# A sandwich block on one core: the last layer norm's mean folded into the down weights, and a token's two expert rows added by an accumulating transfer

## The chip, the core and the metric

One Trainium2 chip, one of its cores. The metric is the device time of one launch in microseconds (us). TensorE multiplies, VectorE, ScalarE and GpSimd work element by element, SyncE only issues transfers; each of them runs its own list of instructions in order and waits on semaphores for the others. GpSimd can issue transfers too, on a queue of its own.

## The reference

The input is x of 8 batches of 256 rows of 256 channels: 2048 tokens, which the kernel holds as 16 tiles of 128 tokens.

```python
x = x + layernorm(attention(layernorm(x)))       # 16 heads, 4 kv heads, D 128, rope, causal
x = x + layernorm(ffn(layernorm(x)))

# ffn, for each token
probs = softmax(xf @ gate_w.T);  w, idx = top_k(probs, 2);  w = w / w.sum()
h = silu(xf @ w_gate[e]) * (xf @ w_up[e])        # 8 experts, 176 wide
out = sum over the two chosen e of w_e * (h_e @ w_down[e])
out += sigmoid(xf @ shgate_w) * (silu(xf @ shw_gate) * (xf @ shw_up) @ shw_down)   # shared, 352 wide

layernorm(y) = (y - mean(y)) / sqrt(var(y) + 1e-5)
```

Everything is float32. The last step of the output is thus a layer norm over the 256 channels of the sum of three rows (two experts' and the shared one), added to x.

## The kernel before

Matmuls run in float32 replaced by three products of high and low parts (`mm3`, L468 to L472). The work has four stages.

1. Attention, up to about 480 us. A loop over steps s = 0 to 128 (`WOVEN`) writes each engine's order out; a step holds one head of one batch, and even and odd steps alternate between a light and a heavy part of the projection and rope. 16 steps are a batch. GpSimd applies rope (L1982, L1985, L1992), VectorE the other element-wise work. SyncE fills the table `xs` with zeros meanwhile, loads the shared weights `sw` and, as their places come free, the experts' weights `ew` (`load_ew`, L425), gate, up and down of an expert in one transfer; the down part of the shared weights is the third part of `sw` (L423).
2. Shared expert for tiles 0 to 10 ("U" items), and the scatter of every token's row to the two lists of its experts.
3. Routed experts: 39 tiles ("R" items) of 128 listed rows. Each result row is multiplied by its weight (L1138) and scattered by GpSimd to `ys` (L2105), where the first and the second choice of a token lie next to each other (1 KB each).
4. The tail, from 634 us. TensorE computes the shared expert of tiles 11 to 15: `u_gate`, `u_up`, `u_T`, `u_down`. ScalarE multiplies the result by the token's gate (`u_out`, L1101). When the last rows of `ys` have landed, SyncE loads eight pairs of tiles, each with both choices (L453 to L457, 512 KB each). For pairs 0 to 4 GpSimd adds the choices (`last_ysum`, L2108) and VectorE the shared rows (`last_sum`, L1709). For pairs 5, 6 and 7 TensorE adds all three in PSUM by multiplying with the identity (`pair_results`, L766; `pair_shared`, L777). VectorE takes mean and variance (`last_stats`, L1716, then `norm_aggr`), GpSimd the reciprocal root and the negative mean times root (`last_root`, L2039), ScalarE applies both (`last_apply`, L1140; for pair 7 VectorE, L1729), VectorE adds to x (L1740, L1735), and SyncE stores (L460, L463).

The order in stages 3 and 4 comes from `ffn(q)`, one function for each engine (L782, L1147, L1743, L2113), called for item after item; `PAIR`, `PPE` and `PSUM` say at which item which pair is treated.

Of the kernel before, what the change touches and what calls it, by code (L numbers as in the profile page):

```python
# [11 lines left out]
NB = 8  # L12
# [5 lines left out]
NE = 8  # L18
# [41 lines left out]
YRING = 4  # L60


U0 = 139
# [17 lines left out]
PAIR = {U1 + 3 + p: p for p in range(NPAIR)}  # L81
SEND = U1 + 3 + NPAIR + 4

PPE = 5
PSUM = U1 + NT - UFIRST + 1
# [30 lines left out]
def program(nc, x_d, wqkv_d, wo_d, gb_d, sw_d, ew_d, cs_d, const_d, route_d, spare_d, out_d):  # L116
    with ExitStack() as ctx:
# [14 lines left out]

        def part(t, at, n):
            return t[:, at:at + n]
# [31 lines left out]
        rs = sb("rs", [128, 2, 5])  # L166
        half = sb("half", [128, 8])
# [36 lines left out]

        ew_raw = [part(ropes, z * EH, EH) for z in range(3)]
# [8 lines left out]
        for c, (a, b) in enumerate(CHUNKS):  # L214
# [62 lines left out]
                for (a, b), p in zip(CHUNKS, (pQ[:, 768:1024], pS[1], pS[1]))]  # L277
# [9 lines left out]
        pSum = [pS[1], pA, pT]  # L287
# [8 lines left out]
        s_dsw, s_droute, s_zeroed = sem("s_dsw"), sem("s_droute"), sem("s_zeroed")  # L296
        s_dew = [sem(f"s_dew{z}") for z in range(2)]
# [3 lines left out]
        s_dyl = [sem(f"s_dyl{p}") for p in range(NPAIR)]  # L301
        s_out = sem("s_out")
# [17 lines left out]
        s_shared, s_y, s_fapp = (sem(n) for n in ("s_shared", "s_y", "s_fapp"))  # L320
# [24 lines left out]
        s_add, s_mul, s_rope, s_swlo, s_shalf, s_zrow, s_weq, s_wsel, s_ysum = (  # L345
            sem(n) for n in ("s_add", "s_mul", "s_rope", "s_swlo", "s_shalf", "s_zrow", "s_weq",
                             "s_wsel", "s_ysum"))
# [20 lines left out]
        def root_of(p):  # L368

            return p // 2 if p < 6 else p - 3  # L370
# [18 lines left out]
        block = ctx.enter_context(nc.Block())  # L389

        @block.sync
        def _(e):
# [18 lines left out]
            e.dma_start(rc, route_d).then_inc(s_droute, 16)  # L411
            e.wait_ge(s_zrow, 1)
# [8 lines left out]
            e.dma_start(part(stage, UB, 2 * SHUP), sw_d[:, 0:2 * SHUP]).then_inc(s_dsw, 16)  # L421
            e.wait_ge(s_swlo, 2)
            e.dma_start(sw_raw[2], sw_d[:, 2 * SHUP:]).then_inc(s_dsw, 16)  # L423

            def load_ew(x):  # L425
                if x >= 2:
                    e.wait_ge(s_dew[x % 2], 16 * (x // 2))
# [39 lines left out]
        def _(e):  # L467
# [298 lines left out]
            def pair_results(p):  # L766
                e.wait_ge(s_dyl[p], 16)
                if p == PPE:
                    e.wait_ge(s_y, NRT)
                elif p == PPE + 1:  # L770
                    e.wait_ge(s_rlo, NRT)
                else:
                    e.wait_ge(s_usilu, NT)
                e.matmul(pair_row[p], ident, yl[p][:, :, 0:HID], start=True, stop=False, skip_group_check=True)
                e.matmul(pair_row[p], ident, yl[p][:, :, HID:2 * HID], start=False, stop=False, skip_group_check=True)

            def pair_shared(p):  # L777
                e.wait_ge(s_shared, 2 * p + 2)
                e.matmul(pair_row[p], ident, shpair[p].rearrange("p (t c) -> p t c", t=2), start=False, stop=True,
                         skip_group_check=True).then_inc(s_psum, 1)  # L780

            def ffn(q):  # L782
# [4 lines left out]
                if q == U1:  # L787
                    r_T(h)
                    r_down(g)
                    r_down(h)  # L790
                elif kind == "U":
                    u_gate(i)
                if q == PSUM:
                    pair_results(PPE)
                if before2 == "U" and q > U1:
                    u_down(g)
                if before == "U" and q > U1:
                    u_T(h)
                if kind == "U":
                    u_up(i)  # L800
# [8 lines left out]
                if q == U1 - 1:  # L809
                    u_gate(UFIRST)  # L810
                if q == PSUM:
                    pair_shared(PPE)
                    for p in range(PPE + 1, NPAIR):
                        pair_results(p)
                        pair_shared(p)
# [134 lines left out]
            for q in range(R0 + 1, SEND):  # L950
                ffn(q)

        @block.scalar
        def _(e):
# [85 lines left out]
            def ew_hi(x):  # L1040
                e.wait_ge(s_dew[x % 2], 16 * (x // 2 + 1))
# [59 lines left out]
            def u_out(m):  # L1101
# [4 lines left out]
                elif m == 14:  # L1106
                    e.wait_ge(s_shalf, 2)
# [32 lines left out]
            def last_apply(p):  # L1140
                e.wait_ge(s_nb2, NB + root_of(p) + 1)
# [1152 lines left out]
```

## Time and profile before

| | us |
|---|---|
| three runs | 671.63, 672.00, 673.67 |
| median | 672.0 |
| the profiled execution: its own time | 673.56 |
| the profiled execution: its span, first to last instruction | 671.8 |

| engine | busy us | share of the span |
|---|---|---|
| TensorE (PE) | 631.1 | 94% |
| ScalarE (ACT) | 551.3 | 82% |
| VectorE (DVE) | 549.9 | 82% |
| GpSimd (POOL) | 530.5 | 79% |

The profile names engines PE, PEld (TensorE's weight load), DVE, ACT, POOL and SP; SPq is SyncE's transfer queue; L12 is line 12 of the kernel. An instruction's duration overlaps with its follower's beginning, so that the step from one start to the next is shorter than the duration.

### The profile page before, as it was taken

How to read it: one execution, taken by the hardware profiler on the slowest of the kernel's cores; microseconds unless marked ns; L12 is line 12 of the kernel's file. 1: busy time of each engine (PE TensorE's matmuls, PEld its weight loads, DVE VectorE, ACT ScalarE, POOL GpSimd, SP SyncE). 2: the span in 40 equal slices, each digit the busy share in tenths (PEclk: the TensorE clock that was granted, in tenths of full speed). 3: DMA queues.
4: the chain of work that ended last, by engine and by line, in shares of the span. 5: the costliest groups of instructions: out<-in, count | busy, mean ns of one | idle time of the engine just before them, and what ended most of it. 6: DMA issues, size and time to landing. Idle time of an engine off the chain costs nothing.

```text
span 671.8 us, 15617 instructions
## 1 busy us (share of the span) xinstructions
PE 631.1 (94%) x4506; PEld 586.9 (87%) x4506; DVE 549.9 (82%) x1912; ACT 551.3 (82%) x2105; POOL 530.5 (79%) x601
## 2 busy tenths in 40 slices
PE   5879999999999999999999999999789989999993
PEld 5657899999999999999999999999678889999991
DVE  3989999898898889899898999979878755555466
ACT  3589999999999999999999999999787536666633
POOL 3698898999899899989989998999757424666664
PEclk9999999999999999999999999999899999999997
DMA  8001306997740000000000000000526033444173
GB/s 328 33 0 33 104 1 198 335 335 209 4 47 1 1 1 1 1 1 2 1 1 1 1 1 2 1 1 25 160 101 229 33 90 111 128 130 119 67 265 125
DMA packets 51122, 54.27 MB, mean 81 GB/s; under 512 B 19840, under 2 KB 42752, under 8 KB 50912
## 3 DMA queue, kind: packets, MB, share of 16 engines
q1 hardware_dynamic: 47632, 43.90, 23.6%
q0 software_dynamic: 3408, 9.38, 3.7%
q8 instruction: 39, 0.64, 0.4%
q14 instruction: 43, 0.35, 0.2%
HBM read 23.83 MB, written 29.51 MB: 79 GB/s over the span
## 4 chain that ended last, share of the span: by engine, by line
PE 75%; DVE 9%; POOL 5%; issue 4%; ACT 4%; DMA 2%; POOLq 0%; SPq 0%; ACTq 0%; DVEq 0%
PE pQ L470 8%; PE pQ L471 8%; PE pQ L472 8%; PE pPO L576 5%; PE pPO L470 5%; PE pPO L472 5%; PE pPO L471 5%; PE pT L548 4%; PE pSS L470 3%; PE pA L470 3%; PE pA L471 3%; PE pA L472 3%; PE pSS L471 2%; PE pSS L472 2%; POOL xs L2076 2%
## 5 line engine op out<-in xcount | busy, mean ns | idle before, releaser
L1002 ACT ACTIVATE P<-P,nmx 128x128 f32<-128x128 f32 (+1 forms) x256 | 118.8, 491 | 1.0 <-DVE nmx L1445 1.0
L470 PE MATMUL pQ<-W 128*128 128x512 f32 (+2 forms) x334 | 116.1, 347 | 2.4 <-DVE W L1359 1.2
L471 PE MATMUL pQ<-W 128*128 128x512 f32 (+2 forms) x334 | 111.6, 334 | 0.0
L472 PE MATMUL pQ<-W 128*128 128x512 f32 (+2 forms) x334 | 111.3, 333 | 0.0
L1982 POOL TENSOR_TENSOR ropes<-ropes 128x640 f32<-128x640 f32 x63 | 99.3, 1576 | 13.7 <-DVE ropes L1422 13.4
L1010 ACT ACTIVATE P<-P,rinv 128x128 f32<-128x128 f32 (+1 forms) x256 | 105.8, 481 | 2.1 <-DVE rinv L1451 2.1
L1992 POOL TENSOR_TENSOR ropes<-ropes 128x640 f32<-128x640 f32 x63 | 99.6, 1580 | 4.9
L470 PE MATMUL pPO<-W 128*128 128x256 f32 (+1 forms) x323 | 95.3, 295 | 5.6 <-DVE W L1460 3.9
L987 ACT ACTIVATE ropes<-pQ 128x128 f32<-128x128 f32 x320 | 88.4, 303 | 9.7 <-PE pQ L472 9.7
L471 PE MATMUL pPO<-W 128*128 128x256 f32 (+1 forms) x323 | 92.0, 285 | 0.0
L472 PE MATMUL pPO<-W 128*128 128x256 f32 (+1 forms) x323 | 91.8, 284 | 0.0
L1455 DVE TENSOR_TENSOR W<-pPO,W 128x384 fp32r<-128x384 f32 x128 | 70.2, 548 | 23.5 <-ACT W L1015 23.4
L1985 POOL TENSOR_TENSOR ropes<-ropes,rs 128x640 f32<-128x640 f32 x63 | 80.3, 1274 | 4.9
L1968 POOL TENSOR_TENSOR rs<-rs,half 128x5 f32<-128x5 f32 x64 | 76.0, 1187 | 5.3
L987 ACT ACTIVATION_READ_ACCUMULATOR ropes<-pQ 128x1 f32 x320 | 74.8, 237 | 0.0
L470 PEld LDWEIGHTS pPO<-W 128*128 128x128 f32 x323 | 62.0, 192 | 12.0 <-DVE W L1460 6.1
L470 PEld LDWEIGHTS pQ<-W 128*128 128x128 f32 x334 | 63.4, 190 | 6.6 <-DVE W L1359 1.6
L1015 ACT ACTIVATE W<-pPO 128x384 fp32r<-128x384 f32 x128 | 65.9, 515 | 2.9 <-PE pPO L576 2.9
L472 PEld LDWEIGHTS pQ<-W 128*128 128x128 f32 x334 | 63.2, 189 | 5.6
L1432 DVE TENSOR_TENSOR W<-pT,W 128x384 fp32r<-128x384 f32 (+1 forms) x128 | 61.6, 481 | 5.6 <-ACT W L995 5.5
L2105 POOL DMA_INDIRECT ys<-ropes x39 | 38.8, 995 | 34.2 <-ACT ropes L1138 28.7
L471 PEld LDWEIGHTS pQ<-W 128*128 128x128 f32 x334 | 63.4, 190 | 2.6
(272 smaller groups left out, 2170.5 us busy)
## 6 DMA issues: line engine op xcount, KB each, us to landing
xs<-stage SPq DMA_DIRECT2D x1, 17550.0 KB, 58.4
stage<-xs SPq DMA_DIRECT2D x39, 130.0 KB
ropes<-in_ew SPq DMA_DIRECT2D x8, 608.0 KB
stage<-in_wqkv SPq DMA_DIRECT2D x3, 768.0 KB, 9.0
stage<-ys SPq DMA_DIRECT2D x4, 512.0 KB, 7.3
ropes<-ys SPq DMA_DIRECT2D x4, 512.0 KB, 6.8
out<-X SPq DMA_DIRECT2D x7, 256.0 KB, 2.0
X<-in_wo SPq DMA_DIRECT2D x1, 1536.0 KB, 12.7
```

The costliest lines, as they stand in the source:

```text
L470: e.matmul(out, lh, rh, start=start, stop=False, skip_group_check=True)
L471: e.matmul(out, lh, rl, start=False, stop=False, skip_group_check=True)
L472: return e.matmul(out, ll, rh, start=False, stop=stop, skip_group_check=True)
L987: a = e.activation(t2[:, z, h * D:h * D + D], pQ[:, h * D:h * D + D], ACT.Square, accum_out=ss[:, z, h:h + 1])
L1002: a = e.activation(P[:, z, span(t)], P[:, z, span(t)], ACT.Exp, bias=nmx[:, z, t:t + 1], scale=-1.0, accum_out=sums[:, z, t:t + 1])
L1010: a = e.activation(P[:, z, span(t)], P[:, z, span(t)], ACT.Copy, scale=rinv[:, z, t:t + 1])
L1015: e.activation(PT[:, 0, n % 2, :], pP[:, 0:384], ACT.Copy).then_inc(s_PThi, 1)
L1455: e.tensor_tensor(PT[:, 1, n % 2, :], pP[:, 0:384], f(PT[:, 0, n % 2, :]), ALU.subtract).then_inc(s_PT, 1)
L1968: e.tensor_tensor(dst, dst, half[:, 0:n], ALU.pow).then_inc(s_root, 1)
L1982: e.tensor_tensor(t1[:, z3, :], t1[:, z3, :], t2[:, z, :], ALU.add).then_inc(s_add, 1)
L1985: e.tensor_tensor(v3, v3, rs[:, z, :].unsqueeze(2).to_broadcast([128, 5, D]), ALU.mult).then_inc(s_mul, 1)
L1992: e.tensor_tensor(v3, v3, TB[:, t, :, :], ALU.add).then_inc(s_rope, 1)
```

## The change

1. Down weights without a mean. SyncE loads the down weights of the shared expert (parts of 512 and 256 columns) and of the eight experts (512 columns) one part at a time into a free piece of `ropes`; VectorE takes the sum of each row of 256 (`down_mean`, steps 48, 56, ..., 120) and subtracts sum/256 (`down_centre`, steps 50, 58, ..., 122); SyncE writes the part to a new table `downs` in device memory. `load_ew` is now two transfers for each expert, gate and up from the input, down from `downs`, and the third part of `sw` comes from `downs` as well. Each row of the sum of the three results then has the mean zero, and the last layer norm needs only the mean of squares.
2. The choices. SyncE loads the first choices of a pair (256 rows of 1 KB), and GpSimd issues a transfer which adds the second choices to them (`second_choice`, `accum_op=ALU.add`), in the order 0, 1, 2, 3, 6, 4, 7, 5. The transfer o waits for the transfer o-2 to land. GpSimd's sums (`last_ysum`) are gone.
3. Pairs 6 and 7 on TensorE. The token's gate is multiplied in by VectorE before the down product (`u_act`), `u_down` of tiles 12 to 15 writes straight into the pair's PSUM bank, and one identity product adds the choices. Pairs 0 to 5 take the shared rows by VectorE.
4. The norm. ScalarE squares the pair's rows with an accumulated sum (`last_square`), GpSimd takes the root in four groups (pairs 0-1, 2-3, 4-6, 7), VectorE does x + row * root in one instruction for each tile (`last_add`). `last_stats`, `last_apply` and `last_scale` are gone.
5. The tail's order is written out as a list for every engine, from item `U1`.

```diff
+CHOICE = (0, 1, 2, 3, 6, 4, 7, 5)
+
+
+DOWN = [(NE, 0, 2 * HID), (NE, 2 * HID, NKT * HID)] + [(x, EA, EH) for x in range(NE)]
+DOWN_SUM = {48 + 8 * c: c for c in range(len(DOWN))}
+DOWN_SUB = {50 + 8 * c: c for c in range(len(DOWN))}
...
-PAIR = {U1 + 3 + p: p for p in range(NPAIR)}
-SEND = U1 + 3 + NPAIR + 4
-
-PPE = 5
-PSUM = U1 + NT - UFIRST + 1
+PPE = 6
+NSUM = 2 * PPE
...
-        pSum = [pS[1], pA, pT]
+        pSum = [pS[1], pA]
...
-            return p // 2 if p < 6 else p - 3
+            return min(p // 2, 2) if p < NPAIR - 1 else 3
...
+        def choice_rows(p, k):
+            return ys_d[4 * 128 * p:4 * 128 * (p + 1), :].rearrange("(t p k) c -> p t k c", t=2, k=2)[:, :, k, :]
+
+        def wait_choices(e, p):
+            o = CHOICE.index(p)
+            e.wait_ge(s_dyl2[o % 2], 16 * (o // 2 + 1))
...
+            def load_down(c):
+                x, a, b = DOWN[c]
+                src = ew_d[:, x * EH + a:x * EH + b] if x < NE else sw_d[:, 2 * SHUP + a:2 * SHUP + b]
+                e.dma_start(down_raw[c % 2][:, 0:b - a], src).then_inc(s_ddown, 16)
+
+            load_down(0)
...
+            for c in range(len(DOWN)):
+                x, a, b = DOWN[c]
+                at = 2 * x * HID + (a if x == NE else 0)
+                e.wait_ge(s_down, 2 * c + 1)
+                if c > 0:
+                    e.wait_ge(s_sdown, 16 * c)
+                if c + 1 < len(DOWN):
+                    load_down(c + 1)
+                e.wait_ge(s_down, 2 * c + 2)
+                e.dma_start(downs_d[:, at:at + b - a], down_raw[c % 2][:, 0:b - a]).then_inc(s_sdown, 16)
             e.wait_ge(s_swlo, 2)
-            e.dma_start(sw_raw[2], sw_d[:, 2 * SHUP:]).then_inc(s_dsw, 16)
+            e.wait_ge(s_sdown, 16 * len(DOWN))
+            e.dma_start(sw_raw[2], downs_d[:, NE * 2 * HID:]).then_inc(s_dsw, 16)
...
-                e.dma_start(ew_raw[x % 3], ew_d[:, x * EH:(x + 1) * EH]).then_inc(s_dew[x % 2], 16)
+                e.dma_start(ew_raw[x % 3][:, 0:EA], ew_d[:, x * EH:x * EH + EA]).then_inc(s_dew[x % 2], 16)
+                e.dma_start(ew_raw[x % 3][:, EA:EH], downs_d[:, x * 512:x * 512 + 512]).then_inc(s_dew[x % 2], 16)
...
-            for p in range(NPAIR):
-                if p == 6:
-                    e.wait_ge(s_hU, NOWN)
-                e.dma_start(yl[p], ys_d[4 * 128 * p:4 * 128 * (p + 1), :].rearrange(
-                    "(t p k) c -> p t (k c)", t=2, k=2)).then_inc(s_dyl[p], 16)
+            e.wait_ge(s_hU, NOWN)
+            for p in CHOICE:
+                e.dma_start(yl[p][:, :, 0:HID], choice_rows(p, 0)).then_inc(s_dyl[p], 16)
...
-                else:
+                elif m < NSUM:
                     e.wait_ge(s_shared, m)
                 if m == UFIRST:
                     e.wait_ge(s_y, NRT)
+                elif m == NSUM + 2:
+                    e.wait_ge(s_rlo, NRT)
+                out = pair_row[m // 2][:, m % 2, :] if m >= NSUM else pD
                 for k in range(NKT):
-                    p = mm3(pD, [aTs[m % 2][:, i, k * 128:k * 128 + 128] for i in range(2)],
-                            [shdown_w(i, k) for i in range(2)], k == 0, k == NKT - 1)
+                    p = mm3(out, [aTs[m % 2][:, i, k * 128:k * 128 + 128] for i in range(2)],
+                            [shdown_w(i, k) for i in range(2)], k == 0 and (m < NSUM or m % 2 == 0), k == NKT - 1 and m < NSUM)
...
             def pair_results(p):
+                wait_choices(e, p)
+                e.matmul(pair_row[p], ident, yl[p][:, :, 0:HID], start=False, stop=True,
                          skip_group_check=True).then_inc(s_psum, 1)
 
...
+            u_gate(15)
+            u_down(13)
+            u_T(14)
+            u_up(15)
+            u_T(15)
+            u_down(14)
+            pair_results(6)
+            u_down(15)
+            pair_results(7)
...
-            def last_apply(p):
-                e.wait_ge(s_nb2, NB + root_of(p) + 1)
+            def last_square(p):
+                if p < PPE:
+                    e.wait_ge(s_fsum, p + 1)
+                else:
+                    e.wait_ge(s_psum, p - PPE + 1)
+                if p < 4:
+                    e.wait_ge(s_nb2, NB)
+                else:
+                    e.wait_ge(s_lr2, NB + root_of(p - 4) + 1)
                 for t in range(2):
-                    a = e.activation(yl[p][:, t, 0:HID], pair_row[p][:, t, :], ACT.Identity, bias=nb2[:, p % 4, t:t + 1],
-                                     scale=lr2[:, p % 4, t:t + 1])
-                a.then_inc(s_fapp, 1)
-
-            def ffn(q):
+                    a = e.activation(yl[p][:, t, HID:2 * HID], pair_row[p][:, t, :], ACT.Square,
+                                     accum_out=mv2[:, p % 4, t, 1:2])
+                a.then_inc(s_ssq, 1)
...
+            u_silu(14)
+            u_hi(13)
+            last_square(0)
+            u_silu(15)
+            u_hi(14)
+            last_square(1)
+            u_hi(15)
+            last_square(2)
+            last_square(3)
+            last_square(4)
+            last_square(5)
+            last_square(6)
+            last_square(7)
...
+            def down_rows(c):
+                x, a, b = DOWN[c]
+                return down_raw[c % 2][:, 0:b - a].rearrange("p (k d) -> p k d", d=HID), (b - a) // HID
+
+            def down_mean(c):
+                rows_c, n = down_rows(c)
+                e.wait_ge(s_ddown, 16 * (c + 1))
+                e.tensor_reduce(down_sum[:, c, 0:n], rows_c, AXX, ALU.add).then_inc(s_down, 1)
+
+            def down_centre(c):
+                rows_c, n = down_rows(c)
+                e.wait_ge(s_down, 2 * c + 1)
+                e.scalar_tensor_tensor(rows_c, down_sum[:, c, 0:n].unsqueeze(2).to_broadcast([128, n, HID]), -1.0 / HID,
+                                       rows_c, ALU.mult, ALU.add).then_inc(s_down, 1)
...
-                e.tensor_tensor(actb[m % 2][:, 0:NSH], sgb[m % 2], pU, ALU.mult).then_inc(s_uact, 1)
+                if m < NSUM:
+                    e.tensor_tensor(actb[m % 2][:, 0:NSH], sgb[m % 2], pU, ALU.mult).then_inc(s_uact, 1)
+                else:
+                    e.wait_ge(s_shalf, 1 if m < 14 else 2)
+                    e.scalar_tensor_tensor(actb[m % 2][:, 0:NSH], sgb[m % 2], sgate[:, m:m + 1], pU, ALU.mult,
+                                           ALU.mult).then_inc(s_uact, 1)
...
             def last_sum(p):
-                e.wait_ge(s_ysum, p + 1)
+                wait_choices(e, p)
                 e.wait_ge(s_shared, 2 * p + 2)
                 e.tensor_tensor(yl[p][:, :, 0:HID], yl[p][:, :, 0:HID], shpair[p].rearrange("p (t c) -> p t c", t=2),
                                 ALU.add).then_inc(s_fsum, 1)
-                e.wait_ge(s_fsum, p + 1)
-
...
+            def last_add(p):
...
+                    x = X[:, 2 * p + t, :]
+                    a = e.scalar_tensor_tensor(x, pair_row[p][:, t, :], lr2[:, p % 4, t:t + 1], x, ALU.mult, ALU.add)
+                    if t == 1 or p == NPAIR - 1:
+                        a.then_inc(s_fres, 1)
...
+            u_lo(13)
+            last_sum(0)
+            u_act(14)
+            last_sum(1)
+            u_lo(14)
+            u_act(15)
+            last_sum(2)
+            u_lo(15)
+            last_sum(3)
+            last_add(0)
+            last_add(1)
+            last_sum(4)
+            last_sum(5)
+            last_add(2)
+            last_add(3)
+            last_add(4)
+            last_add(5)
+            last_add(6)
+            last_add(7)
...
             def last_root(p, n):
                 k = NB + root_of(p)
                 if p >= 4:
-                    e.wait_ge(s_fapp, p + n - 4)
+                    e.wait_ge(s_fres, p + n - 4)
                 else:
                     e.wait_ge(s_h2row, NT)
                 z = slice(p % 4, p % 4 + n)
-                e.wait_ge(s_aggr2, NB + p + n)
-                e.tensor_scalar(lr2[:, z, :], mv2[:, z, :, 1], 1.0, EPS, ALU.mult, ALU.add).then_inc(s_var2, 1)
-                if p < NPAIR - 1:
-                    e.tensor_scalar(nb2[:, z, :], mv2[:, z, :, 0], -1.0, None, ALU.mult)
+                e.wait_ge(s_ssq, p + n)
+                e.tensor_scalar(lr2[:, z, :], mv2[:, z, :, 1], 1.0 / HID, EPS, ALU.mult, ALU.add).then_inc(s_var2, 1)
                 e.wait_ge(s_var2, k + 1)
                 e.tensor_tensor(lr2[:, z, :], lr2[:, z, :], half[:, 0:2 * n].rearrange("p (a b) -> p a b", a=n),
                                 ALU.pow).then_inc(s_lr2, 1)
-                if p < NPAIR - 1:
...
-            def last_ysum(p):
+            def second_choice(p):
+                o = CHOICE.index(p)
                 e.wait_ge(s_dyl[p], 16)
-                e.tensor_tensor(yl[p][:, :, 0:HID], yl[p][:, :, 0:HID], yl[p][:, :, HID:2 * HID],
-                                ALU.add).then_inc(s_ysum, 1)
-
-            def ffn(q):
+                if o >= 2:
+                    e.wait_ge(s_dyl2[o % 2], 16 * (o // 2))
+                e.dma_start(yl[p][:, :, 0:HID], choice_rows(p, 1), accum_op=ALU.add).then_inc(s_dyl2[o % 2], 16)
+
...
+            for p in CHOICE:
+                second_choice(p)
+            last_root(0, 2)
+            last_root(2, 2)
+            last_root(4, 3)
+            last_root(7, 1)
...
```

## Rows read from the trace of the kernel before

**Rows 1.** Windows of the span: length, then busy us per engine, clock, DMA share, GB/s.

```profile
core 0: us, PE busy (x) PEld busy (x) DVE busy (x) ACT busy (x) POOL busy (x), PEclk, DMA share, GB/s
...
140.00:420.00 280.00, 280.00 (x2072) 265.09 (x2071) 251.52 (x941) 268.47 (x1124) 257.42 (x271) 1.00 0.17 30
...
660.00:672.00 12.00, 1.06 (x3) 0.19 (x1) 6.64 (x17) 3.16 (x7) 5.06 (x10) 0.63 0.36 131
```

**Rows 2.** Timeline of VectorE in the attention stage: start us, us, what, idle before.

```profile
117.78 0.75 DVE L1470 BATCH_NORM_STATS2 st<-osb 128x6 f32<-128x256 f32 x2
...
202.94 0.75 DVE L1335 BATCH_NORM_STATS2 st<-X 128x6 f32<-128x256 f32 x2
203.72 0.25 DVE L1339 BATCH_NORM_AGGREGATE mv<-st 128x2 f32<-128x6 f32 x2
...
207.63 0.69 DVE L1460 TENSOR_TENSOR W<-pA,W 128x512 fp32r<-128x512 f32 x1 [0.67 <-ACT W L1021]
```

**Rows 3.** Waits within 140 to 420 us: in total us, times, longest.

```profile
POOL ropes L1982 <- DVE ropes L1422: 4.8, 5, 1.1
```

**Rows 4.** VectorE line L1464 (duration ns min/median/max), and timelines at 67 and 205 us.

```profile
L1464 DVE TENSOR_TENSOR W<-X,W x8: 680/1326/1661, 47.7 to 75.1; 128x512 fp32r<-128x512 f32 x8
...
67.48 1.33 DVE L1464 TENSOR_TENSOR W<-X,W 128x512 fp32r<-128x512 f32 x1
...
68.34 1.59 POOL L1985 TENSOR_TENSOR ropes<-ropes,rs 128x640 f32<-128x640 f32 x1
...
205.51 1.26 POOL L1985 TENSOR_TENSOR ropes<-ropes,rs 128x640 f32<-128x640 f32 x1
```

**Rows 5.** Timeline of SyncE's DMA queue: start us, us to issue, what.

```profile
182.87 4.69 SPq L421 DMA_DIRECT2D stage<-in_sw  x1
454.40 0.33 SPq L423 DMA_DIRECT2D stage<-in_sw  x1
```

**Rows 6.** The chain that ended last, its tail: start us, us, what.

```profile
637.86 2.41 DMA ys<-ropes
...
640.36 3.61 DMA stage<-ys
```

**Rows 7.** GpSimd line L2105: duration ns min/median/max, first and last start us.

```profile
L2105 POOL DMA_INDIRECT ys<-ropes x39: 954/961/1097, 560.9 to 637.9; - x39
```

**Rows 8.** Windows of the tail, columns as in Rows 1.

```profile
646.00:652.00 6.00, 5.68 (x42) 5.37 (x42) 5.83 (x16) 1.91 (x6) 5.92 (x5) 1.00 1.05 393
```

**Rows 9.** Timeline of GpSimd in the tail.

```profile
651.50 0.52 POOL L2047 TENSOR_SCALAR lr<-mv 128x4 f32<-128x4 f32 x1
...
652.30 1.04 POOL L2051 TENSOR_TENSOR lr<-lr,half 128x4 f32<-128x4 f32 x1
```

**Rows 10.** Timeline of VectorE in the tail.

```profile
647.50 0.51 DVE L1557 TENSOR_TENSOR stage<-stage,pSS 128x352 f32<-128x352 f32 x1
...
653.39 0.68 DVE L1712 TENSOR_TENSOR ropes<-ropes 128x512 f32<-128x512 f32 x1
...
666.94 0.76 DVE L1735 TENSOR_TENSOR X<-X,stage 128x256 f32<-128x256 f32 x2
```

**Rows 11.** Timeline of TensorE in the tail.

```profile
648.83 0.49 PE L687 MATMUL pPO<-const,stage 128*128 128x128 f32 x3
...
654.89 1.02 PE L779 MATMUL pSS<-P,const 128*128 128x512 f32 x2
```

**Rows 12.** Timeline of ScalarE: activations with an accumulated sum, 256 and 128 columns.

```profile
201.07 0.51 ACT L1002 ACTIVATE P<-P,nmx 128x256 f32<-128x256 f32 x1
...
201.57 0.80 ACT L1010 ACTIVATE P<-P,rinv 128x128 f32<-128x128 f32 x2
202.26 0.27 ACT L987 ACTIVATE ropes<-pQ 128x128 f32<-128x128 f32 x1
...
202.51 0.28 ACT L987 ACTIVATE ropes<-pQ 128x128 f32<-128x128 f32 x1
```

**Rows 13.** SyncE line L460, the result's seven stores of a pair: us to landing.

```profile
DMA to landing us min/median/max: 2.0/2.0/2.2
```

More of the change, by code:

```diff
@@ L202, in program @@
         rw_raw = rc[:, 215:215 + 2 * NR].rearrange("p (k r) -> p k r", k=2)
+        down_raw = [part(ropes, 2304 + 512 * z, 512) for z in range(2)]
         ew_raw = [part(ropes, z * EH, EH) for z in range(3)]
@@ L301, in program @@
         s_dyl = [sem(f"s_dyl{p}") for p in range(NPAIR)]
+        s_dyl2 = [sem(f"s_dyl2{p}") for p in range(2)]
         s_out = sem("s_out")
@@ L319, in program @@
                              "s_rhi"))
-        s_shared, s_y, s_fapp = (sem(n) for n in ("s_shared", "s_y", "s_fapp"))
+        s_shared, s_y, s_ssq = (sem(n) for n in ("s_shared", "s_y", "s_ssq"))
         s_bn, s_aggr, s_hrow, s_hT, s_wqlo, s_tab_d, s_rope_d = (
@@ L786, in ffn @@
                 after, k = item(q + 1)
[L787 to L800, printed above, removed]
                 if after == "R":
@@ L808, in ffn @@
                         r_down(g)
[L809 to L815, printed above, removed]
             centre(0)
@@ L949, in _ @@
             u_down(10)
-            for q in range(R0 + 1, SEND):
-                ffn(q)
+            for q in range(R0 + 1, U1):
+                routed(q)
+            u_gate(11)
+            r_T(NRT - 1)
+            r_down(NRT - 2)
+            r_down(NRT - 1)
+            u_up(11)
+            u_gate(12)
+            u_T(11)
+            u_up(12)
+            u_gate(13)
+            u_down(11)
+            u_T(12)
+            u_up(13)
+            u_gate(14)
+            u_down(12)
+            u_T(13)
+            u_up(14)
+            u_gate(15)
[7 more added lines that the diff above has]
+            pair_results(7)
         @block.scalar
@@ L1326, in _ @@
             u_out(10)
-            for q in range(R0 + 1, SEND):
-                ffn(q)
+            for q in range(R0 + 1, U1):
+                routed(q)
+            r_out(NRT - 3)
+            r_hi(NRT - 1)
+            u_silu(11)
+            r_out(NRT - 2)
+            r_out(NRT - 1)
+            u_silu(12)
+            u_hi(11)
+            u_silu(13)
+            u_out(11)
+            u_hi(12)
+            u_silu(14)
[11 more added lines that the diff above has]
+            last_square(7)
         @block.vector
@@ L1746, in ffn @@
                 after, k = item(q + 1)
-                if q == U1:
-                    r_lo(h)
-                if q in PAIR:
-                    if PAIR[q] < PPE:
-                        last_sum(PAIR[q])
-                    last_stats(PAIR[q])
-                if before == "U" and q > U1:
-                    u_lo(h)
-                if kind == "U":
-                    u_act(i)
                 if after == "R":
@@ L1762, in ffn @@
                     r_act(i)
-                p = PAIR.get(q - 2, 0)
-                if 0 < p < 6 and p % 2 == 1:
-                    last_add(p - 1)
-                    last_add(p)
-                elif p == 6:
-                    last_add(p)
-                elif p == 7:
-                    last_scale(p)
-                    for t in range(2):
-                        last_add_tile(p, t)
             ln1_stats(0)
@@ L1957, in _ @@
             r_act(0)
-            for q in range(R0 + 1, SEND):
-                ffn(q)
+            for q in range(R0 + 1, U1):
+                routed(q)
+            r_lo(NRT - 1)
+            u_act(11)
+            u_lo(11)
+            u_act(12)
+            u_lo(12)
+            u_act(13)
+            u_lo(13)
[17 more added lines that the diff above has]
+            last_add(7)
         @block.gpsimd
@@ L2219, in _ @@
             r_select(0)
-            for q in range(R0 + 1, SEND):
-                ffn(q)
+            for q in range(R0 + 1, U1):
+                routed(q)
+            r_out(NRT - 3)
+            r_out(NRT - 2)
+            r_out(NRT - 1)
+            for p in CHOICE:
[4 more added lines that the diff above has]
+            last_root(7, 1)
 def kernel(**inputs):
```

95 lines of the change are left out of this document (16 added, 79 removed).

## The prediction

> **What bounds the kernel now.** I read the windows of the whole span first. The reader is to see that between 140 and 420 us TensorE has no idle time (280.00 of 280) while VectorE is busy for 251.5 us of it and GpSimd for 257.4, and that after 660 us TensorE works 1.06 us of 12 [rows 1]. So the kernel is bound by TensorE nearly to the end, and then by a chain through the other engines, which the chain of waits shows: GpSimd's last scatter at 637.86 lands at 640.27, the first pair (512 KB) is issued at 640.36 and landed 3.61 us later [rows 6], and VectorE's last addition runs from 666.94 to 667.70 [rows 10]. After it come only the last stores and the end of the program. Nothing else of the change can shorten the time: it lies in the tail, and what it adds earlier must be hidden under TensorE. So I ask two things: what the added work costs before 634 us, and when VectorE's last addition would end.
>
> **Added in the attention stage.** A step lasts 3.55 us: the statistics at 117.78 belong to step 30 and those at 202.94 to step 54, so 85.16 us are 24 steps [rows 2]. The first sum (step 48) is then due at 182 us, the last centring (step 122) at 444 us. Ten row sums and ten centrings, nine of each on 512 columns. For a sum I take 0.6 us, the 0.69 of a 512-column operation of VectorE less its overlap [rows 2]. A centring reads two operands from on-chip memory; the nearest row is L1464, 512 columns with both operands there, at 0.68 to 1.66 us, median 1.33 [rows 4]. Ten times 0.6 and 1.33 are 19 us at most, against 280 less 251.5, that is 28.5 us, of idle VectorE. Is it idle in the right place? Step 54 carries statistics and aggregates of 1.0 us, and in the pair of steps behind them VectorE still waits 0.67 us for ScalarE [rows 2]: a pair has room for 1.67, and sum and centring go to different pairs. Both fit, a centring of 1.66 just so. The ends of this cost: 0 if all is hidden; if nothing of the centrings' second half could be caught up on (each 1.66 less 0.67), 10 us. I take 0.2 us, near nothing, because extras of 1.0 us leave TensorE at 280 of 280.
> GpSimd pays too. Beside the L1464 at 67.48 its multiplication at 68.34 took 1.59 us [rows 4]; the same instruction at 205.51 took 1.26 [rows 4], so a centring costs GpSimd some 0.3 us, ten of them 3 us. Over 280 us GpSimd waited for VectorE five times, 4.8 us in all [rows 3]. That cover is just enough; where it is gone, rope comes late and TensorE waits for it (a rival, below).
> The Trainium skill bears on this (page "SBUF — State Buffer", section "Who interferes with whom"): a VectorE instruction with two SBUF inputs contends with a GpSimd instruction that reads SBUF, while on trn2 a tensor_reduce never does. The row agrees for the first half (1.33 against 0.68 us); no row here shows the second. By the page the ten sums are free for GpSimd and the ten centrings aren't, which speaks against the second half of this part alone, and leaves the sum as it is.
>
> **SyncE's queue.** The first part is loaded before the zero fill. The second is issued behind the shared weights, whose issue ends at 182.87 + 4.69 = 187.6 us [rows 5], and is wanted at step 56, 210 us: hidden. Later loads and stores (256 KB; a store of that size lands in 2.0 us [rows 13]) have 28 us for each part. The last part is centred at 444 to 446 us and stored by 449; the load of the third part of the shared weights, which now waits for that store, is issued at 454.40 anyway [rows 5], because it waits for GpSimd's split. So this new wait has 5 us of slack. The split of the experts' loads adds eight issues of under 0.5 us where nobody waits for these loads. 0.
>
> **Removed from the tail.** GpSimd's five sums, seven of TensorE's nine identity products, all statistics and aggregates of VectorE, ScalarE's eight pairs of applications but for eight pairs of squares, GpSimd's negated means. What is late next is the second choices.
>
> **The chain of the accumulating transfers.** The first load is now 256 KB. The half that falls away takes 262 KB / 393 GB/s = 0.67 us at the rate of this stretch [rows 8], so it lands at 640.36 + 3.61 - 0.67 = 643.3. GpSimd then issues with g each, and a transfer lands R after its issue begins. Since transfer o waits for o-2, they go two by two in four rounds: the sixth lands at 643.3 + g + 3R, and GpSimd has issued the eighth at 643.3 + 2g + 3R. GpSimd's roots stand behind these eight issues in its list, and VectorE's last_add(0) and (1), which need the first root, stand before last_sum(4): so the whole end of the tail hangs on that moment.
> For g I take 0.96 us, as an indirect scatter of 128 rows takes [rows 7]; with 256 rows it could be double, 1.9. For R no row of before has an accumulating transfer. From below: a scatter of 128 KB lands 2.41 us after GpSimd begins it [rows 6]. From above: g and a load of 512 KB, since the transfer has to read both addends, 0.96 + 3.61 = 4.57 [rows 6, 7]. (Below nothing it can't go: it is time until data land.) I take the middle, 3.5, as neither row is nearer: the one has half the bytes, the other both addends' bytes and a neighbour in the queue. Then GpSimd is free at 643.3 + 1.9 + 10.5 = 655.7.
> From there: root of pairs 0-1, 1.5 us (651.50 to 653.34, less the 0.3 us of the negated mean) [rows 9]: 657.2. Four additions of 256 columns at 0.38 (two in 0.76) [rows 10]: 658.7. last_sum(4), 0.7 [rows 10]: 659.4. ScalarE's squares: with accumulated sum 256 columns step 0.50 us from on-chip memory (201.07 to 201.57), 128 columns from PSUM 0.25 (202.26 to 202.51) [rows 12], so I take 1.0 us for each of pairs 4 and 5 and 0.75 for pair 6: 662.2. Root of pairs 4 to 6, 1.5: 663.7. Eight additions for pairs 4 to 7, 3.0: 666.7. Six handovers of 0.05: 667.0. Pair 7's own square and root (0.75 and 1.2) run beside these additions. Before, it was 667.70: 0.7 us gained. Four pairs now store within 3 us, where each store alone takes 2.0 us [rows 13]: I add 0.2 us. Sum: -0.7 + 0.2 + 0.2 = -0.3 us on the span of 671.8.
> Does the earlier part hold? last_sum(0) stands before u_act(14) in VectorE's list and now waits for the first accumulating transfer, 643.3 + 3.5 = 646.8, done 647.5; u_act(14) began at 647.50 and TensorE came for it at 648.83 [rows 10, 11]. With R above 4.3 TensorE is held up; by then the chain above is later still, so it adds nothing. TensorE's list ends with pair_results(7), whose transfer lands at 643.3 + 4R = 657.3; before, TensorE had its last u_down done at 654.89 [rows 11] and the rest of its sums by 661. Not on the path.
>
> **In the metric.** The profiled execution took 673.56 us, its span 671.8, and the median of the three runs is 672.0; the difference of -0.3 us is laid on the median: 671.7 us. Within 0.3% (2.0 us) a measurement of this kernel can't tell a change from none; so this is a forecast of no measurable change, 0.42, with a range of its own from 670.2 to 673.2 (R from 3.0 to 4.0).
>
> **Rivals.**
> A. Short rounds, 0.30. The transfers behave like the small scatter, R = 2.4. For it: two are in flight at once, and nothing else needs the transfer engines after the loads. Against it: twice the bytes, and a read of the destination. 3 x 1.1 = 3.3 us less: 668.4 us, faster. The Trainium skill has a price here (page "DMA: Bandwidth & Descriptors", section "Anatomy of one DMA — SWDGE (gpsimd) path"): about 2.0 us plus bytes / 436e9, thus an estimate of 2.6 us for 256 KB. By that price the sum would be 669.0 us. The trace's scatter, 2.41 us with 128 KB, agrees; that page has no accumulation in this price.
> B. Long rounds, 0.20. R = 4.57, because the engines read the sum's place too or the issue of 256 rows takes 1.9 us. For it: every microsecond of R counts three times, of g twice. Against: only the upper rows have it. 3.2 us more: 674.9 us; with the long issue 676.8. It decides from R = 4.3 on (2.0 us over no change).
> C. The attention stage isn't hidden, 0.08. GpSimd's 3 us of contention fall where it had no wait (five waits for ten centrings), rope is late, TensorE waits: 674.9 us. Against: the windows show TensorE without idle time beside GpSimd at 257.4 of 280.
>
> **The numbers.** The predicted time is the likeliest case's, 671.7. Faster by over 0.3%: A and a little of the main case, 0.33. Within: 0.40, the main case with a small part of B and C less what it gives to either side. Slower: the rest of B and C, 0.27. The range, 8 in 10, reaches down to A's 668.4 less a little, and up to halfway between B's two values: 668.0 to 676.0.
>
> **What would show it.** GpSimd's eight issues two by two, the distance from the first of a round to the next is R; the first root begins at about 655.7; VectorE waits before last_add(0) and ends near 667.0. TensorE's windows from 180 to 440 us stay without idle time and its steps keep 3.55 us; the centrings show 0.7 to 1.7 us. The load of the shared down part stays at about 454 us. I am wrong if the rounds aren't two by two in effect (the loads late, the issue long), if the first root isn't what VectorE waits for, or if the routed stage begins later than before.

## The result and the profile after

| | kernel before | kernel after |
|---|---|---|
| median, us | 672.84 (4 runs, 671.63 to 677.22) | 683.84 (4 runs, 681.51 to 683.97) |
| ratio, 95% interval | | 1.0146 [1.0119, 1.0172] |
| span of the profiled execution, us | 671.8 | 682.0 |

Slower by 1.5%, above the range that was forecast. The spans differ by 10.2 us, and the tail holds nearly all of it. The first view is SyncE's timeline: the loads of the first choices begin at 641.79 us, where those of before began at 640.36 [rows 6], 1.43 us later.

```profile
641.79 0.91 SPq L489 DMA_DIRECT2D stage<-ys  x2
...
645.29 0.47 SPq L489 DMA_DIRECT2D ropes<-ys  x1
...
668.18 8.44 SPq L492 DMA_DIRECT2D out<-X  x7
```

GpSimd's timeline of the same stretch holds the eight issues of the accumulating transfers (L2152; x2 is two in one row) and behind them the roots. The brackets give the idle time before a row and what ended it.

```profile
644.64 2.58 POOL L2152 DMA_DIRECT2D stage<-ys  x2 [4.46 <-DMA stage<-ys]
652.96 1.18 POOL L2152 DMA_DIRECT2D ropes<-ys  x1 [5.74 <-DMA stage<-ys]
655.03 1.19 POOL L2152 DMA_DIRECT2D ropes<-ys  x1 [0.89 <-DMA stage<-ys]
657.95 1.18 POOL L2152 DMA_DIRECT2D stage<-ys  x1 [1.72 <-DMA ropes<-ys]
659.97 1.19 POOL L2152 DMA_DIRECT2D ropes<-ys  x1 [0.85 <-DMA ropes<-ys]
662.61 1.18 POOL L2152 DMA_DIRECT2D stage<-ys  x1 [1.45 <-DMA stage<-ys]
664.64 1.20 POOL L2152 DMA_DIRECT2D ropes<-ys  x1 [0.85 <-DMA ropes<-ys]
665.92 0.19 POOL L2091 TENSOR_SCALAR lr<-mv 128x4 f32<-128x4 f32 x1
```

The reader is to see four rounds of two. From the first round to the second it is 8.3 us, from there on 5 and 4.7; the root begins at 665.92. The chain that ended last runs through exactly these transfers (start, us, what):

```profile
641.79 2.55 DMA stage<-ys
644.34 0.30 issue
644.64 0.84 POOL stage L2152
645.47 9.05 DMA stage<-ys
...
654.56 0.47 issue
655.03 4.43 DMA ropes<-ys
...
659.50 0.47 issue
659.97 4.15 DMA ropes<-ys
...
664.64 1.19 POOL ropes L2152
```

VectorE waits 7.09 us for that root and ends at 676.18 + 0.86 = 677.04, where it ended at 667.70 before [rows 10]:

```profile
652.46 0.69 DVE L1767 TENSOR_TENSOR stage<-stage,ropes 128x512 f32<-128x512 f32 x1 [4.17 <-DMA stage<-ys]
...
667.27 1.67 DVE L1774 SCALAR_TENSOR_TENSOR X<-stage,lr,X 128x256 f32<-128x256 f32 x4 [7.09 <-POOL lr L2093]
...
676.18 0.86 DVE L1774 SCALAR_TENSOR_TENSOR X<-pA,lr,X 128x256 f32<-128x256 f32 x2
```

From SyncE's first load of the choices to VectorE's end it is 35.25 us, before 27.34. I call this the interval and use it below, since it does not depend on when the tail begins, which differs by some us from chip to chip. It repeats well: experiment 2, whose tail is the same, has 35.58 us in another batch. The 10.2 us are then 1.43 (the loads begin later), 7.91 (the interval) and 0.86 (from VectorE's end to the end of the span, 4.96 against 4.1).

### The profile page after: what moved, and what is told of

It is laid out like the page before. It is cut to its first block, busy times and chain, and to the rows that moved or that the text cites. A ratio compares the mean times of both kernels' runs of the same rounds, so it can differ in the third digit from the quotient of the medians.

```text
span 682.0 us, 15628 instructions
## 1 busy us (share of the span) xinstructions
PE 630.0 (92%) x4492; PEld 586.9 (86%) x4492; DVE 554.8 (81%) x1906; ACT 550.4 (81%) x2119; POOL 532.2 (78%) x594
## 3 DMA queue, kind: packets, MB, share of 16 engines
q1 hardware_dynamic: 51664, 46.79, 23.9%
## 4 chain that ended last, share of the span: by engine, by line
POOL 46%; PE 26%; issue 9%; DVE 9%; DMA 5%; ACT 3%; POOLq 0%; SPq 0%; DVEq 0%; ACTq 0%
POOL ropes L2026 10%; POOL ropes L2036 9%; POOL ropes L2029 8%; POOL rs L2012 8%; PE pQ L502 3%; PE pQ L504 3%; PE pQ L503 3%; POOL xs L2115 3%; POOL lr L2012 2%; DMA stage<-ys 2%; PE pPO L502 1%; PE pT L758 1%; PE pA L786 1%; PE pPO L503 1%; DMA ropes<-ys 1%
## 5 line engine op out<-in xcount | busy, mean ns | idle before, releaser
L502 PE MATMUL pPO<-W 128*128 128x256 f32 (+1 forms) x311 | 91.3, 294 | 5.6 <-DVE W L1497 4.3
L503 PE MATMUL pPO<-W 128*128 128x256 f32 (+1 forms) x311 | 88.3, 284 | 0.0
L504 PE MATMUL pPO<-W 128*128 128x256 f32 (+1 forms) x311 | 88.0, 283 | 0.0
L2012 POOL TENSOR_TENSOR rs<-rs,half 128x5 f32<-128x5 f32 x64 | 78.4, 1225 | 5.3
L1492 DVE TENSOR_TENSOR W<-pPO,W 128x384 fp32r<-128x384 f32 x128 | 69.9, 546 | 12.9 <-ACT W L1043 11.3
L502 PEld LDWEIGHTS pPO<-W 128*128 128x128 f32 x311 | 59.4, 191 | 11.5 <-DVE W L1497 6.9
L608 PE MATMUL pPO<-const,P 128*128 128x128 f32 x384 | 63.2, 274 | 4.1 <-DVE W L1492 3.9
```

The source lines that it names most:

```text
L502: e.matmul(out, lh, rh, start=start, stop=False, skip_group_check=True)
L503: e.matmul(out, lh, rl, start=False, stop=False, skip_group_check=True)
L504: return e.matmul(out, ll, rh, start=False, stop=stop, skip_group_check=True)
L1492: e.tensor_tensor(PT[:, 1, n % 2, :], pP[:, 0:384], f(PT[:, 0, n % 2, :]), ALU.subtract).then_inc(s_PT, 1)
L2012: e.tensor_tensor(dst, dst, half[:, 0:n], ALU.pow).then_inc(s_root, 1)
```

## The experiments

Two batches, each on a chip of its own with the kernel before beside it (673.78 us, 13 runs, and 669.55 us, 17 runs).

**1. The engines add, all else as after.** SyncE loads both choices of a pair in one transfer, GpSimd adds pairs 0 to 5, TensorE two identity products for 6 and 7.

```diff
...
-                e.dma_start(yl[p][:, :, 0:HID], choice_rows(p, 0)).then_inc(s_dyl[p], 16)
+                e.dma_start(yl[p], ys_d[4 * 128 * p:4 * 128 * (p + 1), :].rearrange(
+                    "(t p k) c -> p t (k c)", t=2, k=2)).then_inc(s_dyl[p], 16)
...
-                e.dma_start(yl[p][:, :, 0:HID], choice_rows(p, 1), accum_op=ALU.add).then_inc(s_dyl2[o % 2], 16)
+                e.tensor_tensor(yl[p][:, :, 0:HID], yl[p][:, :, 0:HID], yl[p][:, :, HID:2 * HID],
+                                ALU.add).then_inc(s_ysum, 1)
...
```

> The changed kernel with its accumulating transfers taken out: SyncE loads both choices of a pair (512 KB, as before), GpSimd adds them for pairs 0 to 5, TensorE by a second identity product for pairs 6 and 7; centring, squares, roots and lists stay. Theory (the accumulating transfers are what is late: the first lands 8 us after its issue, each round lasts 4.4 us): GpSimd is free at about 653 instead of 665.8, VectorE ends 11.1 us behind the first root, at about 664 instead of 677; the time is some 10 us or more below the changed kernel, thus 3 to 6 us below the kernel before. Rival (the new chain behind the roots, squares and additions, is what costs): no more than 3 us below the changed kernel.

Measured: 673.52 us (672.3 to 675.4), ratio 1.0002 [0.9983, 1.0021]. GpSimd's timeline has the six sums and the root at 655.52, SyncE's loads begin at 640.79 and VectorE ends at 665.79 + 0.87 = 666.66: an interval of 25.87.

```profile
644.65 2.65 POOL L2153 TENSOR_TENSOR stage<-stage 128x512 f32<-128x512 f32 x2 [5.46 <-DMA stage<-ys]
647.35 2.97 POOL L2153 TENSOR_TENSOR ropes<-ropes 128x512 f32<-128x512 f32 x2
...
654.08 1.36 POOL L2153 TENSOR_TENSOR ropes<-ropes 128x512 f32<-128x512 f32 x1 [1.38 <-DMA ropes<-ys]
655.52 0.20 POOL L2095 TENSOR_SCALAR lr<-mv 128x4 f32<-128x4 f32 x1
```

So the whole loss hangs on the accumulating transfers: 35.25 - 25.87 = 9.4 us of the interval, and by the two ratios (1.0146 and 1.0002) 9.7 us of the time. The other half of the expectation, 3 to 6 us under the kernel before, did not come: GpSimd is free at 655.52, not at 653. The rest of the change shows no gain in sum. Its tail is 1.5 us shorter (27.34 to 25.87); in the profile 0.4 us of that are lost by a later start of the loads (640.79 against 640.36) and 0.2 us at the end, and the rest is within what the two medians can tell (0.2% to either side, 1.3 us).

**2. No centring** (output keeps the weights' mean). The ten loads, sums, centrings and stores are left out, and the weights loaded straight.

```diff
...
-                if s in DOWN_SUM:
-                    down_mean(DOWN_SUM[s])
-                if s in DOWN_SUB:
-                    down_centre(DOWN_SUB[s])
...
```

> The changed kernel without the centring: down weights are loaded as they are, nothing is summed, subtracted or stored to the table (so the last norm leaves the mean out of account). Theory: the 1.4 us by which the tail begins later (641.79 against 640.36) are the price of the centring under the attention stage; the time falls by 1 to 2 us against the changed kernel. Rival (the start of the tail differs from run to run by that much, since 0.5 us of it are there at 52 us, before any centring): within 0.5 us.

Measured: 683.38 us (681.63 to 684.91), ratio 1.0142 [1.0106, 1.0179]. The centring is not the cause. Its own cost is seen in the time from the second load of `wo` to the first load of an expert, two issues of SyncE's queue that stand in every kernel:

```profile
52.72 0.33 SPq L419 DMA_DIRECT2D X<-in_wo  x1
...
475.83 0.33 SPq L466 DMA_DIRECT2D ropes<-in_ew  x1
```

That is 423.11 us after, 421.97 before, and 422.03 without the centring: 1.1 us. It repeats: the six other kernels with a centring have 422.98 to 423.16 us. The time of the whole kernel did not show it: here the stretch from there to the tail's loads took 167.99 us against 165.96, and a confidence interval of 0.4% to either side (2.5 us) cannot tell 1.1 us. Of the 1.43 us by which the tail's loads began later after than before, 0.48 are there at 52 us already, before any centring (52.72 against 52.24).

**3. Paced loads.** SyncE issues the loads of the second round only when the first accumulating transfer has landed, and the last four loads together when the third has.

```diff
-            for p in CHOICE:
+            for o, p in enumerate(CHOICE):
+                if o >= 2:
+                    e.wait_ge(s_dyl2[0], 16 * ((o - 2) // 2 + 1) if o < 4 else 32)
```

> The changed kernel, SyncE loads only the first choices of pairs 0 and 1 at first, the next two once the first accumulating transfer has landed, the last four once the third has. Theory (packets of GpSimd's queue don't move while SyncE's queue has plain loads waiting): the first accumulating transfer lands 4 to 5 us after its issue instead of 7.8, and the ones issued beside the four last loads are late instead. Rival (the first two are slow because two accumulating transfers are issued at once, or because the first use of the queue in this form is slow): 7 to 9 us as before. The whole time isn't better in either case, since loads are later.

Measured, a single run: 685.05 us. With no plain load behind it the first transfer, begun at 642.62, lets SyncE go on at 647.02: 4.4 us, where the same transfer of the same pair took 7.8 after. The chain of waits of this kernel has it so too, and its last row, a transfer beside the four late loads, takes 5.31:

```profile
642.62 4.39 DMA stage<-ys
...
650.69 4.54 DMA ropes<-ys
...
660.04 5.31 DMA ropes<-ys
```

So the long first round is not the nature of the transfer, nor of two being issued at once, which they are here too: it is long because of the plain loads pending beside it. The kernel gains nothing, because the later rounds now wait for their own loads.
The bytes of the two queues in the kernel after agree. Of its answers for 644 to 646, 646 to 648, 648 to 650 and 650 to 652 us (queue: packets, MB, share), GpSimd's queue (q0) has none in the first two, though its first transfer was issued at 644.64:

```profile
q1 hardware_dynamic: 543, 0.53, 98.9%
...
q1 hardware_dynamic: 688, 0.66, 97.6%
...
q1 hardware_dynamic: 494, 0.47, 81.8%
q0 software_dynamic: 26, 0.03, 10.9%
...
q0 software_dynamic: 327, 0.32, 100.2%
q1 hardware_dynamic: 119, 0.11, 20.8%
```

Part of this silence is the transfer's own delay. In experiment 3, with no load beside it, the first packets of q0 (41, 0.04 MB) stand in the answer for 644.6 to 645 us, and none in those for 643.6 to 644.6: 2.0 us behind the issue at 642.62. By that delay q0 would have moved from 646.7 on in the kernel after. In its answers for 646 to 647, 647 to 648 and 648 to 649 us q0 still has nothing, and q1 has 0.35, 0.32 and 0.31 MB. The Trainium skill (page "DMA: Bandwidth & Descriptors", section "Queues, rings and completion order") says that each transfer engine takes the queues it has work for in turn, a packet from each. Between 646.7 and 649 the trace doesn't look like that: nothing in q0, some 0.7 MB through q1, and the measurement decides how such a transfer is to be priced. From 649 to 652 both queues move side by side. Whether the engines passed q0 over or its work reached them late beside the loads, no run here shows.

**4. Plain second choices** (they are loaded beside the first ones and not added). The same queue, bytes, waits and order, without `accum_op`.

```diff
-                e.dma_start(yl[p][:, :, 0:HID], choice_rows(p, 1), accum_op=ALU.add).then_inc(s_dyl2[o % 2], 16)
+                e.dma_start(yl[p][:, :, HID:2 * HID], choice_rows(p, 1)).then_inc(s_dyl2[o % 2], 16)
```

> The changed kernel, GpSimd's transfers without accumulation: they copy the second choices beside the first ones (nothing adds them, so the output lacks the second choices). Theory A (the addition on the way is what makes a round 4.4 us): rounds of about 3.2 us, 1.2 of issue and 2.0 until the data land, tail 4 to 5 us shorter. Theory B (it is the software queue and the wait between issues): rounds stay over 4 us. In both the first round stays late, since the plain loads go first.

Measured, a single run: 680.42 us. GpSimd's timeline has 0.71 us for an issue instead of 1.18, and the view of the line has a landing 3.1 us (least) and 3.5 us (median) after the issue begins, where the accumulating ones took 4.1 and 4.4:

```profile
653.00 0.71 POOL L2152 DMA_DIRECT2D ropes<-ys  x1 [5.62 <-DMA stage<-ys]
654.00 0.71 POOL L2152 DMA_DIRECT2D ropes<-ys  x1 [0.28 <-issue]
656.59 0.71 POOL L2152 DMA_DIRECT2D stage<-ys  x1 [1.88 <-DMA ropes<-ys]
658.14 0.71 POOL L2152 DMA_DIRECT2D ropes<-ys  x1 [0.84 <-DMA ropes<-ys]
```

Without the accumulation a landing is about 0.9 us shorter, half of that being issue; from loads to root it saves 24.13 - 19.76 = 4.4 us in four rounds, as theory A said, while the rounds behind the first take 3.6 to 4.5 us, between A's 3.2 and B's 4. These 0.9 us are not the addition alone: the plain transfers also go in larger packets (118 for 0.41 MB of q0 from 650 to 652 us, in the same stretch after 327 for 0.32 MB), and the two were not tried apart. The greater part of a round is there without it, the late first round too: from 646 to 650 us q0 moved 0.01 MB and q1 1.06, and the first round took 7.2 us against 8.3.

**5. Six in flight.** Transfer o waits for o-6, so that only the last two wait for others.

```diff
...
-                if o >= 2:
-                    e.wait_ge(s_dyl2[o % 2], 16 * (o // 2))
-                e.dma_start(yl[p][:, :, 0:HID], choice_rows(p, 1), accum_op=ALU.add).then_inc(s_dyl2[o % 2], 16)
+                s, before = choice_sem(o)
+                if o >= 6:
+                    e.wait_ge(s, before)
+                e.dma_start(yl[p][:, :, 0:HID], choice_rows(p, 1), accum_op=ALU.add).then_inc(s, 16)
```

> The changed kernel, but six accumulating transfers may be in flight instead of two (transfer o waits for o-6; other semaphores). Theory (two causes: plain loads go first until about 649, and then each round of two pays the software queue's latency and the wait of 0.5 us before the next issue): without the rounds the eight follow each other as fast as the engines move them, 256 KB at 130 to 160 GB/s, 1.6 to 2.0 us each: the last lands at 649 + 13 to 16 = 662 to 665 instead of about 668, GpSimd is free and the first root done some 8 us earlier, so the time falls by 3 to 5 us and stays above the kernel before. Rival (the rounds are the whole cause): the transfers are over by 657, and the time falls by 8 us or more.

Measured: 671.46 us (670.34 to 671.88) beside 669.55, ratio 1.0034 [1.0019, 1.0049]; the interval is 635.79 to 664.99, 29.2 us, 6.05 less than after: more than the 3 to 5 us of the theory, less than the 8 of its rival. So both causes are there. The rounds are the larger one, 6.05 of the 9.4 us, and still it is slower than before. Six of GpSimd's eight issues no longer wait for an earlier one, and the answer for its queue from 648 to 650 us shows why more in flight would not do more:

```profile
638.90 2.58 POOL L2159 DMA_DIRECT2D stage<-ys  x2 [4.72 <-DMA stage<-ys]
641.31 2.61 POOL L2159 DMA_DIRECT2D ropes<-ys  x2
643.62 1.51 POOL L2159 DMA_DIRECT2D stage<-ys  x1
644.56 1.79 POOL L2159 DMA_DIRECT2D ropes<-ys  x1
647.67 1.18 POOL L2159 DMA_DIRECT2D stage<-ys  x1 [1.32 <-DMA stage<-ys]
```

```profile
q0 software_dynamic: 408, 0.39, 123.6%
```

0.39 MB in 2 us are 195 GB/s. The eight second halves are 2.1 MB, thus an estimate of 10.8 us at that rate; before, SyncE's loads moved them at 393 GB/s [rows 8], 5.3 us. The accumulation by transfer thus gives away an estimated 5.4 us of transfer time even without rounds, and of that 3.3 us are seen in the interval (29.2 against experiment 1's 25.87).

**6. The engines add, in another order.** Experiment 1 with three moves: VectorE's last_sum(4) and (5) before last_add(0), TensorE's pair_results(6) before u_T(15), and pair 5 before pair 7 in the loads.

```diff
...
             last_sum(3)
+            last_sum(4)
+            last_sum(5)
             last_add(0)
             last_add(1)
-            last_sum(4)
-            last_sum(5)
...
```

> The kernel of e1_engine_sums (no accumulating transfer) with another order of the tail: VectorE does last_sum(4) and (5) before last_add(0), TensorE adds the choices of pair 6 while it waits for tile 15, the pairs are loaded as 0, 1, 2, 3, 6, 4, 5, 7. Theory (in e1 the squares of pairs 4 to 7 stood behind the first root by VectorE's order alone): VectorE ends about 3 us earlier, near 663.5 instead of 666.7, the time is 2 to 4 us under e1 and under the kernel before (some 670 against 672). Rival (pair 7's products or the last loads bound the end): under 1 us.

Measured: 665.51 us (665.24 to 666.35) beside 669.55, ratio 0.9949 [0.9931, 0.9967]: faster than both kernels. In GpSimd's timeline the third group's root waits for ScalarE 1.09 us, where it waited 3.14 us after and in experiment 1; VectorE ends at 659.51, an interval of 23.9 us, 2.0 less than in experiment 1. The time fell by more, 3.6 us by the two ratios; the rest is within their confidence intervals. The three moves were made together, so which of them brings how much is not shown.

```profile
646.83 2.65 POOL L2153 TENSOR_TENSOR ropes<-ropes 128x512 f32<-128x512 f32 x2 [1.02 <-DMA ropes<-ys]
649.56 0.52 POOL L2095 TENSOR_SCALAR lr<-mv 128x4 f32<-128x4 f32 x1
...
654.40 0.28 POOL L2095 TENSOR_SCALAR lr<-mv 128x6 f32<-128x6 f32 x1 [1.09 <-ACT stage L1180]
```

**7. The centrings earlier.** Experiment 6 with all sums and centrings before step 105, to see whether their 1.1 us is a matter of the steps that they stand in.

```diff
...
-DOWN_SUM = {48 + 8 * c: c for c in range(len(DOWN))}
-DOWN_SUB = {50 + 8 * c: c for c in range(len(DOWN))}
+DOWN_SUM = {s: c for c, s in enumerate((48, 58, 64, 66, 74, 80, 82, 90, 96, 98))}
+DOWN_SUB = {s: c for c, s in enumerate((50, 60, 66, 72, 76, 82, 88, 92, 98, 104))}
...
```

> e6_sums_reordered with the sums and centrings moved: all before step 105, none beside the routing work of steps 108 to 117. Theory (the centring's 1.1 us, by which the experts' first load starts later in every kernel with it, come from the last parts, where VectorE was busy for 36.9 of 40 us and 18.6 of 20): the first load of an expert starts again about 422 us behind the second load of the output weights, as in the kernel before, and the time is up to 1 us under e6. Rival (each centring costs 0.1 us wherever it stands): no change against e6.

Measured: 665.53 us (664.94 to 666.14), ratio 0.9946 [0.9928, 0.9964], the same as experiment 6; the attention stage by the measure of experiment 2 took 422.98 us, against 423.09 there. The place does not matter within the stage. Which part of the centring costs the 1.1 us (VectorE's time, GpSimd's, or the transfers) was not tried alone and stays open.

## Why the prediction was wrong

- **The bound.** Right: the time is set in the tail, and what VectorE waits for there is the first root, behind the eight issues in GpSimd's list. From the root's start to VectorE's end I forecast 11.3 us (655.7 to 667.0), measured 11.1 (665.92 to 677.04): additions, squares and roots were sized well together.
- **The step that failed: the chain of the accumulating transfers.** The form was right, two by two in four rounds; its sizes were wrong. The root was to begin at 655.7 and began at 665.92, 10.2 us later. R was 3.5 with bounds of 2.41 and 4.57. The rounds are R and the next issue's delay, 8.3 and 9.6 us for the first (644.64 to 652.96, 645.47 to 655.03), then 4.9 and 4.7 along the chain. Against 3 x 3.5 the three distances make 9.6 + 4.9 + 4.7 = 19.2 us, 8.7 more; the loads' later start adds 1.4, and the longer issues (g of 1.18, not 0.96) and the small terms the rest.
- **Within R, the first round.** My bounds took the transfer alone or beside its like. I had written that a neighbour in the queue counts, but priced nothing for SyncE's own seven loads behind the first, though the first round runs beside them. Experiment 3 gives the price: 4.4 us without them, 7.8 and 9.0 with them. This term, 3.4 to 4.6 us, is larger than the whole range I gave R.
- **Within R, the later rounds.** Landings of 4.1 to 4.5 lie in my bounds, near the upper one. What I left out is that a waiting issue begins only some 0.5 us after its data landed (the "issue" rows of 0.47 in the chain). R as a distance was therefore 4.7 to 4.9, above the bound. Rival B's mechanism (a longer transfer, a longer issue) is there: the landings come near its 4.57, and 0.9 us of them go with the accumulation (experiment 4). Its price of 674.9 to 676.8 was still too low, since it has neither the first round nor the wake-up. Rival A, by the small scatter's row, was wrong: even a plain transfer of this size took 3.1 us at the least. The Trainium skill's price (page "DMA: Bandwidth & Descriptors", section "Anatomy of one DMA — SWDGE (gpsimd) path"), an estimate of 2.6 us, was too low by the same row.
- **TensorE held up.** I had said that with R above 4.3 TensorE is held and that it adds nothing. It was: VectorE's first sum waits 4.17 us, u_act(14) comes at 653.07 instead of 647.50, and TensorE's timeline has this row:

```profile
653.70 0.90 PE L719 MATMUL pPO<-const,stage 128*128 128x128 f32 x3 [3.54 <-DVE stage L1611]
```

 It was off the path, as the root was later still. It was partly at the lower clock too: the granted clock was 0.50 from 655 to 659 us, while in experiment 1, where TensorE is not held up, it stays at 1.00 from 649 to 659. The identity products of pairs 6 and 7 were done before the squares wanted them.
- **The attention stage.** The centrings were cheaper than I took them: the grouped view by line gives 0.72 us for a centring and 0.65 for a sum, 13.7 us in all.

```profile
L1546 DVE SCALAR_TENSOR_TENSOR ropes<-down_sum,ropes 128x512 f32<-128x512 f32 (+1 forms) x10 | 7.2, 720 | 0.0
L1541 DVE TENSOR_REDUCE down_sum<-ropes 128x2 f32<-128x512 f32 (+1 forms) x10 | 6.5, 653 | 0.0
```

 I laid 0.2 us on the stage and it took 1.1 more. The windows, which I had named as the test, hardly show it: 140 to 420 us keeps 279.98 us of busy TensorE in 280. Busy time was the wrong witness, as the ends of matmuls are modelled in this profile and small gaps need not show; the distance between two fixed instructions is the right one. The contention that I priced at 3 us of GpSimd is there: in the same window it is busy for 259.81 us, against 257.42 before and 257.29 in experiment 2, while its waits for VectorE stay at 4.7 us in five. Rival C is thus a small effect of the right sign, not the cause, and whether the 1.1 us are its doing is not shown. (Its sum has a slip as well: 671.7 + 3 is 674.7, not 674.9.)
- **SyncE's queue.** Right in kind: no step waited for the parts, and the load of the third part of the shared weights waits last for GpSimd's split, as before. The slack was 2.3 us by SyncE's waits, not 5, and the load was issued at 456.32 instead of 454.40, 1.4 us of it beyond the 0.48 that are there at 52 us.
- **The stores.** I added 0.2 us for four pairs storing close together; from VectorE's end to the end of the span it became 0.86.

## What to carry to other kernels

Moving a sum from an engine into a transfer turns a throughput (GpSimd's 1.3 us for a pair) into a latency (4.4 us and 0.5 us of wake-up), and with few in flight the latencies add. Price a transfer of GpSimd's queue with what SyncE has pending at that moment, and bound its rounds by issue, landing and wake-up together. When an edit bundles several parts, time it with the suspected part undone: here the same tail with engine sums and a better order was 0.5% faster than the kernel before.

## What the runs showed of the hardware

- A transfer of GpSimd's queue hardly moved while many plain loads of SyncE's queue were pending: 7.8 to 9.0 us to landing against 4.4 with no load beside it. Its first bytes came 2.0 us behind the issue without loads, and over 4 us behind it with them (issued at 644.64, none up to 649).
- An accumulating transfer of 256 rows of 1 KB was issued in 1.18 us and landed in 4.1 at the least; the plain one 0.71 and 3.1. With six allowed in flight the accumulating ones moved 195 GB/s together.
- TensorE stood idle from 650.2 to 653.7 us, and its granted clock was 0.50 from 655 to 659 us, which is the lower level (1.2 GHz). The windows' clock column (the last but two) has it, with TensorE busy for 3.32 us of 4:

```profile
649.00:653.00 4.00, 1.16 (x10) 0.95 (x8) 0.54 (x1) 0.00 (x0) 0.04 (x1) 1.00 1.09 199
...
655.00:659.00 4.00, 3.32 (x14) 2.87 (x14) 2.49 (x5) 2.06 (x9) 2.24 (x2) 0.50 0.94 129
```
